# Fused attention kernel: full-height norm products, one bank at a time, and new orders of turns

## The reference

```
x = x + tanh(g_xattn) * cross_attention(layernorm(x), ctx)          # 16 heads of 8
x = x + tanh(g_ffn)   * net(layernorm(x))                           # 6 layers
# one layer of net:
q, k, v = split(shift(x) @ Wqkv)                                    # 16 heads of 64
q = rotary(q / |q| * q_scale);  k = rotary(k / |k| * k_scale)       # norm over a head's 64 rows
x = softmax(8 q k' within windows of 32 and the window before) v @ Wo + x
x = W2 (a * gelu(gate)) + x,   a, gate = split(layernorm(shift(x)) @ W1)   # inner size 341
```

## Time and profile before

| | us |
|---|---|
| three timed runs | 2061.7, 2063.63, 2075.56 (median 2063.63) |
| the profiled execution, own time | 2055.98 |
| its span, first to last instruction | 2054.2 |
| TensorE matmul busy in the span | 1901.6 (93%) |
| VectorE, ScalarE, GpSimd busy | 1590.3 (77%), 1046.8 (51%), 901.4 (44%) |
| TensorE's share of the chain that ended last | 69% |

### The profile page before, as it was taken

The page is one execution under the profiler, slowest core; times in us unless marked ns, Lnnn a source line. Parts: engine busy times, 40 slices in busy tenths (PEclk is TensorE's granted clock), DMA queues, the critical chain, the costliest instruction groups (busy, mean ns, idle before and its releaser), DMA issues.

```text
span 2054.2 us, 84918 instructions
## 1 busy us (share of the span) xinstructions
PE 1901.6 (93%) x35408; PEld 1262.4 (61%) x35408; DVE 1590.3 (77%) x3092; ACT 1046.8 (51%) x1879; POOL 901.4 (44%) x1231
## 2 busy tenths in 40 slices
PE   6888866899999999999999999999999999999996
PEld 3444433566666767666766667666667676666764
DVE  4555546778888888888888888888888888887883
ACT  3333332355555555646565555555465655554554
POOL 1000004535455555546464646455454646463541
PEclk7898778999999999999999999999999999999998
DMA  1000004555656564656465656547464656565560
GB/s 67 6 10 28 34 0 70 84 85 77 99 102 98 99 106 69 115 93 104 82 92 84 114 101 93 95 70 128 82 107 78 92 83 120 106 89 88 74 102 22
DMA packets 73332, 166.87 MB, mean 81 GB/s; under 512 B 16592, under 2 KB 23504, under 8 KB 72400
## 3 DMA queue, kind: packets, MB, share of 16 engines
q0 software_dynamic: 36864, 100.71, 36.8%
q1 hardware_dynamic: 36432, 65.68, 12.1%
HBM read 20.57 MB, written 1.05 MB: 11 GB/s over the span
## 4 chain that ended last, share of the span: by engine, by line
PE 69%; DVE 13%; issue 9%; ACT 4%; DMA 3%; POOL 2%; DVEq 0%; SPq 0%; ACTq 0%; POOLq 0%
PE ps L1007 10%; PE ps L1158 8%; PE ps L1050 7%; PE ps L1124 6%; PE ps L1104 6%; DVE big L809 4%; PE ps L1020 4%; PE ps L1117 4%; PE ps L940 4%; DVE big L812 3%; PE ps L1074 3%; PE ps L1148 3%; DMA big<-big 3%; PE ps L1036 3%; PE ps L920 2%
## 5 line engine op out<-in xcount | busy, mean ns | idle before, releaser
L482 POOL DMA_DIRECT2D big<-big x768 | 607.3, 1508 | 40.3 <-issue 24.6
L569 ACT ACTIVATE big<-ps 128x512 f32<-128x512 f32 x384 | 225.3, 600 | 573.1 <-PE ps L1007 569.4
L1007 PE MATMUL ps<-big,wn_sb 128*128 128x256 f32 x1536 | 407.8, 399 | 27.4 <-issue 15.0
L1007 PEld LDWEIGHTS ps<-big,wn_sb 128*128 128x128 f32 x1536 | 271.3, 191 | 112.1 <-DVE big L812 60.7
L820 DVE TENSOR_TENSOR big<-big,ps 128x512 f32<-128x512 f32 x384 | 251.1, 683 | 108.9 <-PE ps L1036 81.8
L809 DVE TENSOR_TENSOR big<-ps,tab 128x512 f32<-128x512 f32 x384 | 258.9, 684 | 36.9 <-ACT big L569 34.0
L473 POOL TENSOR_TENSOR big<-big 128x512 f32<-128x512 f32 x96 | 123.6, 1287 | 347.8 <-ACT big L586 347.8
L812 DVE TENSOR_TENSOR big<-ps,tab 128x512 f32<-128x512 f32 x384 | 257.5, 681 | 0.0
L1158 PE MATMUL ps<-big,wo_sb 128*128 128x256 f32 x768 | 226.1, 397 | 0.0
L448 POOL COPY big<-xs 64x256 f32 x144 | 64.5, 448 | 324.7 <-DVE xs L848 316.0
L1050 PE MATMUL ps<-wn_sb,big 128*64 128x512 f32 x768 | 180.7, 610 | 2.9 <-issue 2.2
(11 more groups left out here) (146 smaller groups left out, 2865.1 us busy)
## 6 DMA issues: line engine op xcount, KB each, us to landing
big<-big POOLq DMA_DIRECT2D x768, 128.0 KB, 5.1
big<-big SPq DMA_DIRECT2D x96, 256.0 KB, 5.0
big<-big SPq DMA_DIRECT2D x96, 192.0 KB, 5.1
wn_sb<-in_wn SPq DMA_DIRECT2D x6, 1024.0 KB, 8.4
wn_sb<-in_wn SPq DMA_DIRECT2D x6, 512.0 KB, 6.2
wo_sb<-in_wo SPq DMA_DIRECT2D x6, 512.0 KB, 3.6
w_sb<-in_w SPq DMA_DIRECT2D x6, 341.0 KB, 2.9
w_sb<-in_w SPq DMA_DIRECT2D x6, 192.0 KB, 3.1
```

Of the source, the lines that this page charges most:

```text
L482: eng.dma_start(rot[to:to + 32, at:at + 4, :], src[32 * r:32 * r + 32], accum_op=ALU.add).then_inc(added[i], 16)
L569: eng.activation(sq[:, two, :], ps[:, i % 2, :].rearrange("p (a t) -> p a t", a=2), ACT.Square).then_inc(sq_d, 1)
L1007: mm = eng.matmul(ps[:, k % 2, a * T:a * T + T], wn_sb[:, u * P:u * P + P], sT, start=True, stop=True)
```

## The change

- `QUAD` and `SLOT` go. Unit `u` now has row group `u % 4` and slot `u // 4`, in the selection matrix, in `head_sums` and in `spread`.
- `spread(n)` fills one bank with two products over all 128 rows of `n_parts`; the selection matrix is zero in the other row groups. `R0` waits for three evicted values, `R1` for four, and from `R2` on `R`n waits for the product `H` two before it alone. Its extra semaphore step (`r_go`) goes. There are eight `R` steps in the plan where there were four.
- `head_sums` makes the same products in plain order and signals once, not twice.
- In cross attention `weigh(0, 6)` moves behind the projections, and pairs of `row_scores` alternate with one step each of `scores` or `weigh`; `scores(7)` becomes the last of them.
- TensorE's, ScalarE's and VectorE's plans have new orders. In TensorE's, `F1` stands ahead of `k0`, `k2` to `k5` lie apart, `F4` moves ahead of `k7`, `R0` stands behind `F5`, and `R7` is the last step of a pass. GpSimd's is unchanged.

```
--- before.py
+++ after.py
@@ -41,11 +41,6 @@
 BIG = 32 * 1024
 
 
-
-QUAD = [u // 2 % 2 + 2 * (u // PAIRS) for u in range(UNITS)]
-SLOT = [u % 2 + 2 * (u // 4 % 2) for u in range(UNITS)]
-
-
 def shape_constants():
 
     f = np.float32
@@ -83,7 +78,7 @@
     rsel = np.zeros((P, UNITS, P), f)
     for u in range(UNITS):
         for c in range(3):
-            rsel[32 * QUAD[u] + 8 * c + 2 * SLOT[u] + p // D, u, p] = 256
+            rsel[32 * (u % 4) + 8 * c + 2 * (u // 4) + p // D, u, p] = 256
     parts = -np.stack([(m // 8 >= 1) & (m < 24), m // 8 == 2], 1).astype(f)
     xones = np.zeros((P, 4, 32), f)
     for j in range(4):
@@ -242,7 +237,7 @@
         sc_d, max_d, sub_d, ex_d, den_d, rinv_d, pt_d, ptev, ov_d, on_d, ot_d, oev, wo_d, x_d, w_go, s_go, vf_free, y2_d, den_h, den_s = (
             sem(n) for n in ("sc_d", "max_d", "sub_d", "ex_d", "den_d", "rinv_d", "pt_d", "ptev", "ov_d", "on_d", "ot_d", "oev",
                              "wo_d", "x_d", "w_go", "s_go", "vf_free", "y2_d", "den_h", "den_s"))
-        chain, nchain, nmid, r_go = sem("chain"), sem("nchain"), sem("nmid"), sem("r_go")
+        chain, nchain, nmid = sem("chain"), sem("nchain"), sem("nmid")
 
         nmean, nxc, nsq, nvar, nva, nln, ny, nxn, nt = (
             sem(n) for n in ("nmean", "nxc", "nsq", "nvar", "nva", "nln", "ny", "nxn", "nt"))
@@ -274,13 +269,13 @@
 
 
         PE_PLAN = [(x_[0], int(x_[1:])) for x_ in """
-            S0 k0 k1 F1 S1 k2 k3 T0 T1 F2 k4 k5 g1 W0 W1 T2 k6 T3 k7 U0 U1 g3 W2 W3 V0 V1 V2 V3 F4 R0 O0 U2 U3
-            O1 R2 F5 O2 O3 R4 O4 O5 F6 O6 R6 O7 F7""".split()]
+            S0 F1 k0 k1 S1 k2 F2 T0 k3 T1 k4 g1 W0 W1 k5 T2 k6 T3 F4 k7 U0 U1 g3 W2 W3 V0 V1 V2 V3 U2 O0 O1 F5
+            R0 O2 O3 R1 R2 U3 O4 R3 R4 O5 F6 R5 O6 R6 O7 F7 R7""".split()]
         ACT_PLAN = [(x_[0], int(x_[1:])) for x_ in """
-            s0 s1 x0 F1 s2 s3 F2 t0 t1 x1 s4 s5 s6 t2 t3 s7 u0 n0 v0 v1 F3 v2 u1 v3 F4 u2 u3 F5""".split()]
+            s0 s1 x0 F1 s2 F2 s3 t0 t1 s4 x1 F3 s5 t2 s6 t3 s7 u0 n0 v0 v1 F4 v2 u1 v3 u2 F5 u3""".split()]
         DVE_PLAN = [(x_[0], int(x_[1:])) for x_ in """
-            X0 X1 D0 D1 c0 c1 d0 d1 X2 X3 c2 d2 c3 d3 D2 D3 f0 Z0 f1 c4 d4 c5 d5 Y0 f2 c6 d6 f3 n0 c7 d7 Z1 N1
-            N2 N3 N4 N5 N6 Y1 H0 H1 H2 H3 F5 H4 H5 F6 H6 e0 H7 F7""".split()]
+            X0 X1 D0 D1 c0 d0 c1 X2 d1 D2 c2 d2 X3 f0 D3 f1 c3 f2 d3 c4 f3 d4 Z0 c5 d5 Y0 c6 d6 n0 c7 Z1 d7 Y1
+            N1 N2 N3 N4 N5 N6 H0 F5 H1 H2 H3 H4 F6 H5 e0 H6 F7 H7""".split()]
         POOL_PLAN = [(x_[0], int(x_[1:])) for x_ in """
             A0 F0 Z0 m0 Z1 m1 m2 m3""".split()]
 
@@ -565,7 +560,7 @@
                         two = slice(2 * (i % 4), 2 * (i % 4) + 2)
                         eng.wait_ge(proj, it * PAIRS + (i + 1))
                         if i >= 4:
-                            eng.wait_ge(sums, it * 4 + 2)
+                            eng.wait_ge(sums, it * 2 + 1)
                         eng.activation(sq[:, two, :], ps[:, i % 2, :].rearrange("p (a t) -> p a t", a=2), ACT.Square).then_inc(sq_d, 1)
                     if kind == "n":
 
@@ -793,7 +788,7 @@
                     eng.wait_ge(fvc, l if isinstance(b, int) else l + 1)
                 for kind, i in share(DVE_PLAN, A, Bh, F, "cdnNH", "XDZYe", "Ff"):
                     if kind == "n":
-                        eng.wait_ge(sums, it * 4 + 4)
+                        eng.wait_ge(sums, it * 2 + 2)
                         eng.tensor_scalar(n_s, ps[:, 2, 0:T], 1e-24, 65536.0, ALU.max, ALU.mult).then_inc(ss_d, 1)
                     if kind == "N":
                         norm_heads(i)
@@ -950,8 +945,6 @@
                 if X3:
                     eng.wait_ge(xo_d, b - 1)
                     eng.matmul(ps[:, 7, 0:T], xw_sb[:, 3, :], xo2, start=True, stop=True).then_inc(xwo, 1)
-                if X2:
-                    weigh(0, 6)
                 if X1:
                     normed_tokens()
                 if X2:
@@ -959,18 +952,15 @@
                 if X1:
                     projections()
                 if X2:
+                    weigh(0, 6)
                     weigh(0, 7)
                     scores(3)
-                    weigh(1, 6)
-                    weigh(1, 7)
-                for n, s in ((0, None), (2, 4), (4, 5), (6, "w"), (8, 6), (12, 7)):
-                    if X2 and s == "w":
-                        weigh(2, 6)
-                        weigh(2, 7)
-                    elif X2 and s:
-                        scores(s)
+                between = ((scores, 4), (weigh, 1, 6), (weigh, 1, 7), (scores, 5), (scores, 6), (weigh, 2, 6), (weigh, 2, 7), (scores, 7))
+                for n, (step, *which) in enumerate(between):
                     if X1:
-                        row_scores(n, n + (4 if n in (8, 12) else 2))
+                        row_scores(2 * n, 2 * n + 2)
+                    if X2:
+                        step(*which)
                 if X2:
                     weigh(3, 6)
                 if X1:
@@ -1013,30 +1003,23 @@
                     if g == 1 and Bh:
                         eng.wait_ge(ss_d, it)
                         eng.wait_ge(x_d, it - 1 + FREE)
-                    for a in range(2):
-                        for n in range(4 * g - 4 + a, 4 * g + 4, 2):
-                            u = ORDER[n]
-                            q = QUAD[u]
-                            mm = eng.matmul(ps[32 * q:32 * q + 32, 2, 0:T], sumsel[:, SLOT[u], :], sq[:, n % 8, :],
-                                            start=g == 1 and a == 0, stop=g == 3 and a == 1, skip_group_check=True)
-                        mm.then_inc(sums, 1)
+                    for n in range(4 * g - 4, 4 * g + 4):
+                        u = ORDER[n]
+                        q = u % 4
+                        mm = eng.matmul(ps[32 * q:32 * q + 32, 2, 0:T], sumsel[:, u // 4, :], sq[:, n % 8, :],
+                                        start=n < 4, stop=n >= 12, skip_group_check=True)
+                    mm.then_inc(sums, 1)
 
                 def spread(n):
-
                     if n == 0:
                         eng.wait_ge(r_d, it + 1)
-                        eng.wait_ge(vev, it * 4 + 4)
+                    if n < 2:
+                        eng.wait_ge(vev, it * 4 + (3 + n))
                     else:
-                        eng.wait_ge(hat_d, it * PAIRS + n)
-                    eng.sem_inc(r_go, 1)
+                        eng.wait_ge(hat_d, it * PAIRS + (n - 1))
                     for a in range(2):
-                        for m in (n, n + 1):
-                            u = 2 * HATS[m] + a
-                            q = QUAD[u]
-                            mm = eng.matmul(ps[:, m % 2, a * T:a * T + T], rselb[32 * q:32 * q + 32, u, :], n_parts[32 * q:32 * q + 32, :],
-                                            start=True, stop=True, skip_group_check=True)
-                            if a == 1:
-                                mm.then_inc(rb, 1)
+                        mm = eng.matmul(ps[:, n % 2, a * T:a * T + T], rselb[:, 2 * HATS[n] + a, :], n_parts, start=True, stop=True)
+                    mm.then_inc(rb, 1)
 
                 def values(j):
                     if j == 0:
```

## The result

Four runs of the changed kernel took 1987.4 to 1993.0 us, median 1990.3 us; four of the kernel before, measured beside it, 2059.9 to 2075.6 us, median 2062.7 us. The ratio is 0.964 with a 95% interval of 0.959 to 0.968: 3.6% faster, 72 us on the medians. A second measurement on another chip gave 0.964 (0.961 to 0.967).

A forecast was written before the change was run, and what follows sets the result against it. TensorE was taken as the bound in the layers, while up to 345 us it waits, partly at the lower clock. Terms of 12 + 4 + 22 = 38 us less gave 2026 us on the median; range 1992 to 2062 us.

The forecast's parts named there:

- the terms of -0.44 and +0.2 us: k4 and k5, each pass: 0.44 us of waiting goes, but 0.1 us each is charged for weights not loaded early.
- V1, R2 and R4: TensorE steps of a layer pass given new waits: V1 about 0.1 us for d7, R2 0.1 and R4 0.4 us.
- the table load: ScalarE's 1.28 us load ahead of evictions that V's banks, O2 and R1 need; 0.3 to 0.7 us to spare.
- The rivals in which the passes gain nothing: Layer passes unchanged: only cross attention gains, 2042 us, chance 0.20; or nothing comes of it, 2060 us, chance 0.09.
- bf16 costs the switch: Spreads: change of data type, not shape, costs 0.2 us at each of six places; slower, 2083 us, chance 0.11.
- the clock's rival: Cross attention's clock rises with the waits gone, 15 us more gained: 2011 us, chance 0.15.
- its three terms: Gains summed: layer passes 12 us, ends of layers 4 us, cross attention 22 us; 38 us less in all.
- a list of terms: Layer pass: gains and new waits summed to -0.24 us, a pass of some 34.3 us, 12 us less over 47.
- the walk: New plans followed through one layer pass, step by step with measured durations: 34.2 us.
- the cushion before H5: Ends of layers: H5 about 1.5 us later, so less waiting for rotated halves; 4 us less, between 0 and 10.
- The base: 38 us off the profiled execution's 2056.0 us gave 2018 us; carried to the median of 2063.6 us, 2026 us.
- the clock's case: Cross attention's clock rises, 2011 us, chance 0.15; with half the new waits absent, 1992 us, the range's low end.

The follow-up runs named there:

- e2_full: The kernel before with only the spread products over all 128 rows, one bank at a time, in the old orders: ratio 0.992, 17 us less.
- e4_layers: The changed kernel with cross attention's old order: ratio 0.9805 to the kernel before, 40 us less than it.
- e1_cross: The kernel before with only cross attention's new order of TensorE's turns: ratio 0.9855, 30 us less.
- e3_rows32: The changed kernel with 32-row spread products and the old head-sum order, still one bank at a time: ratio 0.9868 to before, 47 us more than the changed kernel.
- after_again: The changed kernel itself, unaltered, run again beside its variants: ratio 0.9639 to the kernel before.

## Why the prediction fell short

**The mechanisms held.** A spread product over 128 rows takes 0.11 us, the value taken; the switches of shape went, but for one between R7 and the mask's tile of 64 rows (0.31 us from R7 to S0, 0.22 us elsewhere), which stood between F7 and the mask before; k4 and k5 take 2.03 us together (1.06 and 0.97 us) where they took 2.26 us, as the terms of -0.44 and +0.2 us had it; V1, R2 and R4 wait 0.08, 0.03 and 0.34 us where I had 0.1, 0.1 and 0.4; no other step waits behind the table load; H was not late for S0; cross attention has one new wait at `weigh(3, 6)`, of 1.5 us where I had 1.9. The rivals in which the passes gain nothing, or bf16 costs the switch, fell with e2_full and e4_layers; the clock's rival came true in part, as told below.

**Where the sum fell short, term by term.** The step that failed is the sum's: its three terms were all too small. It left out k2's wait for VectorE and the late landings in the middle of layers, gave the first and the last turn of cross attention and the layers' first, shortened pass too little or nothing, and counted none of the clock.

- *The median pass: -0.24 us taken, -0.53 us measured, 13 us in all.* The spreads gave -0.30 us alone (e2_full), against -0.35 us. So the orders gave -0.23 us, where my terms had them at +0.11 us. I had followed the plan to 34.2 us and then taken 34.3 us from a list of terms that left things out; the walk was closer to the 34.0 us. By the medians of the steps, the list missed about 0.11 us in one wait. The prediction says that k2 finds its bank empty in the new plan, but has no term for it. In the old order k2 starts 0.05 us behind the end of d0 in every pass from the third on, in the new one 0.54 us or more behind it, and it starts 0.11 us earlier. Before (a d0 of 0.68 us, then k2), and the changed kernel:

```profile
1199.02 0.68 DVE L812 TENSOR_TENSOR big<-ps,tab 128x512 f32<-128x512 f32 x1
1199.75 1.99 PE L1007 MATMUL ps<-big,wn_sb 128*128 128x256 f32 x8
```

```profile
1186.69 0.68 DVE L807 TENSOR_TENSOR big<-ps,tab 128x512 f32<-128x512 f32 x1
1187.95 1.13 PE L997 MATMUL ps<-big,wn_sb 128*128 128x256 f32 x4
```

  Another 0.15 us is that V1, R2 and R4 wait for 0.45 us in all and not 0.6 us; the rest, under 0.1 us, is spread over small differences. The step behind S0, too, starts 0.11 us earlier in the new orders, for a cause that the traces don't show, but that is worth nothing: S1 starts 4.33 or 4.34 us after S0 at the median of all twelve traces, as the prediction had it, and its wait for D grows from 0.21 to 0.31 us.
- *The excess: -4 us taken, -13.8 us measured.* The cause, the cushion before H5, was the one named. At the five ends of layers it gave 5.5 us, near the 4 us taken and within the bound of 10. What failed is that only ends of layers were counted: 7.7 us came in passes 28 and 43, in the middle of a layer, where H5 waited 4.3 and 3.6 us in before, and 1.9 us in the first two passes; the others took back 1.3 us. In each late pass the 1.5 us of cushion takes effect, and then R7, which needs H5, stands 1.3 us of F7 behind O7, while R6 stood ahead of both.
- *Cross attention: -22 us taken, -27.9 us measured up to the first scores.* By the starts of the transposes of the maxima, the six loop turns gave 16.2 us, 2.7 us each, where I had 3.1 us each, 18.6 us; the turn ahead of the loop gave 5.6 us instead of 3.1 us; its last turn, which I had at nothing, 4.0 us; the way from there to the first scores 3.4 us, nearly all of it the shortened pass of part A (e1_cross), which I had at nothing, too; and the start cost 1.3 us. The turn ahead of the loop took 37.3 us in before but 35.5 or 35.6 us in the three other kernels with its order, so that 1.7 us of its gain are before's own.
- *The loop's near hit is in part luck.* I had left the clock out of the sum. In the loop, TensorE was at 1.2 GHz for 56, 61, 61 and 73 us in the four kernels with cross attention's old order, and the loop took 195.6, 197.1, 197.3 and 202.3 us: 0.4 us more for each us at that level. In the five with the changed kernel's order it was there for 29 to 36 us, and the loop took 175.8 to 179.6 us: 0.5 us for each. From before to changed the lower level held for 20 us less. An estimate from these numbers is that 8 to 10 of the loop's 16.2 us come with the clock and 6 to 8 us from the order alone, 1.0 to 1.4 us a turn and not 3.1 us. No run holds the clock fixed, and a longer wait both lengthens the loop and lowers the clock. The clock of the whole stage explains little: up to the first S0 the lower level held for 122 us in before, 94 us in e4_layers and 85 us in the changed kernel, and e4_layers, with cross attention's old order, still has its first S0 at 342.8 us.
- *The tail: nothing taken, +3.4 us measured.* It goes with cross attention's order and not with the layers': it lasts 53.9 to 56.7 us in e1_cross and all others with a new order there, and 51.8 to 52.7 us in those with the old one. Why is open.
- *The base.* Carrying the sum to the median as a difference assumed that the profiled executions of both kernels lie alike to their medians. They didn't: before's lay 7 us below its median, the changed kernel's 3 us above.

The range failed with the terms: its low end of 1992 us had the clock's case but neither the late passes at their bound nor the error of the base, all of which pointed the same way. The measured 1990.3 us lies 2 us outside.

## What to carry to other kernels

Where TensorE is full, look for small products whose tile shape differs from their neighbours'. Here the switch cost about 0.1 us on either side, and full height with zeros was faster both with four products in a group (e2_full) and with two (e3_rows32). In a plan with fixed turns, put the first step that needs a long DMA as late as possible, and put no step behind it that others wait for. Where the clock falls in waits, price a wait above its length: here 1.5 us were worth 3.0 us a turn. When a plan has been followed from step to step, forecast from the walk and not from a shorter list of its differences, and give every wait that the walk shows to be gone a term. Follow the first and last turns of each loop as well.

## What the runs showed that I had not expected

- A wait of 1.5 us removed from a turn shortened it by 3.0 us; the granted clock of the stage rose from 0.86 to 0.93.
- Between full products of f32 a bf16 product of 256 columns costs 0.11 us and its neighbours nothing, with a new set of weights for each.
- In cross attention's loop a us at the lower clock level went with 0.4 to 0.5 us more of time, but in the turn ahead of it with next to nothing: 31.7 us with 14.6 us at that level (changed) and with 1.6 us (after_again).
- The last DMA of rotated halves, of one kind and size, landed 6 to 7 us after its issue in most passes and about 9 to 12 us in a few. They are nearly the same few in each kernel, and two of them have no load of weights.
